# Graph and expert layers on one core: the tokens' way into the expert queues, and the experts' first layer

## The reference

```
msgs = layernorm(x)[src] * edge_weight[:, None]
x = x + segment_sum(msgs, dst) @ gnn_W.T + gnn_b
xf = layernorm(x)
probs = softmax(xf @ gate_w + gate_b)          # 8 experts
cw = the two largest of probs, else 0
for e in range(8):
    h = gelu(xf @ W1[e] + b1[e])               # 256 -> 512
    acc += cw[:, e] * (h @ W2[e] + b2[e])      # 512 -> 256
x = x + acc
```

## Time and profile before

| | us |
|---|---|
| median of 3 runs | 2954.43 (2953.14 to 2955.53) |
| profiled execution | 2958.51 |
| its span, first to last instruction | 2956.7 |
| PE busy | 2196.5 |
| POOL busy | 2013.2 |
| DVE busy | 1409.3 |
| ACT busy | 740.5 |

### The profile page before, as it was taken

How to read it: one execution, slowest core, us unless ns; L and a number is a source line. 1 busy time by engine, 2 the same in 40 slices (tenths; PEclk the granted TensorE clock), 3 DMA queues, 4 the chain that set the end, 5 groups by cost and what they waited for, 6 DMA issues and landing times.

```text
span 2956.7 us, 40846 instructions
## 1 busy us (share of the span) xinstructions
PE 2196.5 (74%) x9206; PEld 1482.4 (50%) x9207; DVE 1409.3 (48%) x5982; ACT 740.5 (25%) x1985; POOL 2013.2 (68%) x2107
## 2 busy tenths in 40 slices
PE   3656755984876977966966877978877887776695
PEld 2433533653654655644644654655555555544463
DVE  8855434453453443453454453443555555454422
ACT  3410200330221332321321221322322222222242
POOL 6657777777777777777777777777777777751121
PEclk8777977897988988988988987989998899887798
DMA  9663433443444443445555444434455564542423
GB/s 337 225 237 115 127 116 115 136 126 121 129 139 123 133 126 122 139 147 163 173 165 163 145 131 132 132 118 125 138 168 161 161 194 148 158 131 85 151 86 109
DMA packets 231445, 432.24 MB, mean 146 GB/s; under 512 B 47020, under 2 KB 158542, under 8 KB 228006
## 3 DMA queue, kind: packets, MB, share of 16 engines
q0 software_dynamic: 100368, 275.72, 31.3%
q1 hardware_dynamic: 128246, 144.38, 15.4%
q10 hardware_dynamic: 2592, 9.45, 0.8%
HBM read 326.80 MB, written 102.56 MB: 145 GB/s over the span
## 4 chain that ended last, share of the span: by engine, by line
POOL 50%; issue 20%; PE 15%; DVE 11%; DMA 3%; ACT 1%; ACTq 1%; DVEq 0%; SPq 0%; POOLq 0%
POOL rows L363 40%; POOL slots L391 5%; PE bank L599 5%; POOL results L396 5%; PE bank L685 4%; PE bank L667 3%; DVE spread L976 1%; DMA results<-y_sb,result_i 1%; PE bank L676 1%; DMA got<-results 1%; DVE y_sb L1154 1%; DVE item_t L1124 1%; DVE square_n L1023 1%; DVE pre_bn L932 1%; DVE bn L955 0%
## 5 line engine op out<-in xcount | busy, mean ns | idle before, releaser
L363 POOL DMA_INDIRECT rows<-xhat,src_t x1536 | 1470.0, 957 | 476.4 <-issue 464.4
L599 PE MATMUL bank<-rows,spread 128*80 128x256 f32 x3328 | 910.2, 435 | 324.8 <-issue 160.1
L599 PEld LDWEIGHTS bank<-rows,spread 128*80 128x80 f32 x3328 | 564.1, 175 | 607.6 <-issue 320.4
L685 PE MATMUL bank<-w,hT 128*128 x1848 | 489.1, 411 | 115.3 <-ACT hT L822 66.9
L685 PEld LDWEIGHTS bank<-w,hT 128*128 128x128 f32 x1848 | 366.2, 205 | 229.1 <-issue 180.9
L667 PE MATMUL bank<-w,xiT 128*128 x924 | 452.0, 612 | 11.6 <-ACT xiT L805 2.2
L989 DVE TENSOR_TENSOR acc<-acc,bank 128x160 f32 x208 | 67.0, 322 | 755.4 <-PE bank L589 730.3
L396 POOL DMA_INDIRECT results<-y_sb,result_i x231 | 226.8, 982 | 237.4 <-DVE y_sb L1157 181.3
L976 DVE TENSOR_SCALAR spread<-iota_w,dst_rel,wgt 128x80 f32<-128x80 f32 x1536 | 378.5, 340 | 0.2
L1153 DVE CAST result_i<-xi 128x1 int32 x231 | 35.1, 152 | 620.6 <-PE bank L685 339.1
L822 ACT ACTIVATE hT<-bank,b1T 128x128 f32<-128x128 f32 x924 | 263.4, 367 | 217.8 <-PE bank L676 212.2
(11 more groups left out here) (159 smaller groups left out, 1755.3 us busy)
## 6 DMA issues: line engine op xcount, KB each, us to landing
xi<-slots SPq DMA_DIRECT2D x231, 136.0 KB, 2.7
got<-results SPq DMA_DIRECT2D x97, 256.0 KB
rows<-xhat,src_t POOLq DMA_INDIRECT x1536
x_t<-in_x SPq DMA_DIRECT2D x97, 128.0 KB
x_d<-x_t SPq DMA_DIRECT2D x97, 128.0 KB, 2.3
res<-x_d SPq DMA_DIRECT2D x97, 128.0 KB
out_nodes<-res SPq DMA_DIRECT2D x97, 128.0 KB
w<-in_x SPq DMA_DIRECT2D x12, 1024.0 KB, 12.7
```

The source lines that it names most:

```text
L363: pool.indirect_dma_start(rows[q][:, c, :], None, x if g < RAW else xhat, bass.IndirectOffsetOnAxis(ap=src_t[:, g * CG + c:g * CG + c + 1] ...
L599: done = nc.tensor.matmul(B_SUM[0:W, 0:D], spread[g % 2][:, c, :], rows[q][:, c, :], start=c == 0, stop=c == CG - 1)
L685: done = nc.tensor.matmul(B_Y[:, 0:D], hT[i % 2][:, j, :], w2[:, bass.ds(e, 1), j, :].rearrange("p o f -> p (o f)"), start=j == 0, stop=j ...
```

## The change

Two things change together.

**Sort instead of scatter.** The two indirect sends per tile go. `place` additionally works out, for each tile, where each expert's run begins within the tile's 256 choices sorted by expert, and where it goes in the queues (`run_ends`). `mask_choices` (DVE) makes a 128 x 256 one-hot matrix from a tile's two places per node; `sort` (PE) multiplies it by the tile's rows in two halves, in the bank of `linear`; ACT copies each half; SP stores the 256 sorted rows in one of three staging areas in DRAM and, a turn later, copies 8 runs of 128 rows each (whatever their true length; later rows are overwritten) from DRAM to DRAM, after the previous tile's runs have landed. Mask, sort, stage and runs of a tile stand in four successive turns, one tile per turn.

**First weights per item, as the stationary side.** The first weights of an item's expert are loaded by SP with the item into one of 4 buffers, instead of all 8 experts' once. `up` makes 8 matmuls with a 128 x 128 block of weights as the stationary side and the turned item as the moving side (128 columns), which gives the output already turned, in one of two banks; `copy_h` and `turn_h` go, and `gelu` moves from item a to item b of a step, one step earlier.

To make room, the ring of node columns is 8 tiles instead of 16 and the normalisation has 6 buffers instead of 8.

```diff
-RING = 16
+RING = 8
...
+STAGE = 3 * P
+STAGES = 3
 XI = 6
 XB = 3
+W1B = 4
...
-LBUF = 8
+LBUF = 6
...
-        for _ in range(2 if busy else 4):
-            if send_next < NT and place_at.get(PART_OF[send_next], tau) < tau:
-                t.sends.append(send_next)
-                if send_next == PARTS[PART_OF[send_next]][1] - 1:
-                    sent_at[PART_OF[send_next]] = tau
-                send_next += 1
+        if turns:
+            t.sort, t.stage, t.runs = turns[-1].mask, turns[-1].sort, turns[-1].stage
+        if send_next < NT and place_at.get(PART_OF[send_next], tau + 1) <= tau:
+            t.mask = send_next
+            send_next += 1
+        if t.runs >= 0 and t.runs == PARTS[PART_OF[t.runs]][1] - 1:
+            sent_at[PART_OF[t.runs]] = tau
         open_to = max([sure_items(k) for k in sent_at if sent_at[k] < tau], default=0)
         waiting = open_to - item_next
-        n_steps = (1 + (waiting > 6 and tau % 2 == 0)) if busy else 1 if send_next < NT else 3
+        n_steps = (1 + (waiting > 6 and tau % 2 == 0)) if busy else 1 if NK - 1 not in sent_at else 3
...
-        w1, w2 = sb("w1", [P, NX, KD, H]), sb("w2", [P, NX, KH, D])
+        w1, w2 = sb("w1", [P, W1B, KD, H]), sb("w2", [P, NX, KH, D])
...
-            def send(t):
-                k, n = PART_OF[t], valid_rows(t)
-                pool.wait_ge(routed, k + 1)
-                for c in range(2):
-                    pool.indirect_dma_start(slots, bass.IndirectOffsetOnAxis(ap=slot_i[0:n, t, c:c + 1], axis=0),
-                                            xs[0:n, t % XR, :], None).then_inc(sent[k], 16)
...
+            def store_sorted(t):
+                if t >= STAGES:
+                    sp.wait_ge(runs_in, 16 * NX * (t - STAGES + 1))
+                sp.wait_ge(sorted_ready, 2 * t + 2)
+                sp.dma_start(stages[t % STAGES][0:2 * P].rearrange("(h p) f -> p h f", p=P), sorted_x[t % 2][:]).then_inc(staged[t % STAGES], 16)
+
+            def copy_runs(t):
+
+                k = PART_OF[t]
+                j = t - PARTS[k][0]
+                sp.wait_ge(routed, k + 1)
+                at = loaded_row(sp, run_ends[k % 2][:, j].rearrange("p c e -> p (c e)"))
+                sp.wait_ge(staged[t % STAGES], 16 * (t // STAGES + 1))
+                if t:
+                    sp.wait_ge(runs_in, 16 * NX * t)
+                if t in EPOCH_TILES[1:]:
+                    sp.wait_ge(tails_in, 16 * NX * EPOCH_OF[k])
+                for e in range(NX):
+                    a = nc.s_assert_within(at[e], 0, 2 * P, skip_runtime_bounds_check_because="a sum of a tile's counts")
+                    b = nc.s_assert_within(at[NX + e], 0, NX * S - 2 * P, skip_runtime_bounds_check_because="S holds every token")
+                    sp.dma_start(slots[bass.ds(b, P), :], stages[t % STAGES][bass.ds(a, P), :]).then_inc(runs_in, 16)
...
-                sp.wait_ge(routed, k + 1)
+                sp.wait_ge(runs_in, 16 * NX * PARTS[k][1])
...
-                    wait_sent(sp, k)
+                    sp.wait_ge(runs_in, 16 * NX * PARTS[k][1])
                     if ends_epoch(k):
                         sp.wait_ge(tails_in, 16 * NX * (EPOCH_OF[k] + 1))
...
+                b, e = loaded_row(sp, item_be[:, i])
+                b = nc.s_assert_within(b, 0, NX * BLOCKS - 1, skip_runtime_bounds_check_because="a block of the queues")
+                e = nc.s_assert_within(e, 0, NX - 1, skip_runtime_bounds_check_because="the block's expert")
                 if i >= XI:
                     sp.wait_ge(y_ready, i - XI + 1)
-                at = sp.value_load(item_b[:, i:i + 1], min_val=0, max_val=NX * BLOCKS - 1)
-                sp.dma_start(xi[i % XI][:], blocks[bass.ds(at, 1)].rearrange("o p f -> p (o f)")).then_inc(xi_in[i % XI], 16)
+                sp.dma_start(xi[i % XI][:], blocks[bass.ds(b, 1)].rearrange("o p f -> p (o f)")).then_inc(xi_in[i % XI], 16)
+                if i >= W1B:
...
                 else:
                     pe.wait_ge(x1_ready, t)
+                if n_sorted[0]:
...
+            def sort(t, h):
+                if h == 0:
+                    pe.wait_ge(mask_set, t + 1)
+                pe.wait_ge(x1_ready, n_linear[0])
+                if t or h:
+                    pe.wait_ge(sorted_ready, 2 * t + h)
+                nc.tensor.matmul(B_NODE[:, 0:XW], sort_mask[t % 2][:, h * P:(h + 1) * P], xs[:, t % XR, :],
+                                 start=True, stop=True).then_inc(sort_done, 1)
...
             def up(i):
+                pe.wait_ge(w1_in_sem[i % W1B], 16 * (i // W1B + 1))
+                pe.wait_ge(xiT_ready, i + 1)
+                if i >= 2:
+                    pe.wait_ge(hT_ready, i - 1)
+                for j in range(KH):
+                    for b in range(KD):
+                        done = nc.tensor.matmul(B_H[i % 2][:, j * P:(j + 1) * P], w1[:, i % W1B, b, j * P:(j + 1) * P], xiT[i % 2][:, b, :],
+                                                start=b == 0, stop=b == KD - 1)
+                done.then_inc(h_summed, 1)
...
+                    pe.wait_ge(w_in, 16 * NX)
                 pe.wait_ge(listed, part_of_item(i) + 1)
-                e = pe.value_load(item_e[:, i:i + 1], min_val=0, max_val=NX - 1)
-                pe.wait_ge(xiT_ready, i + 1)
-                if i:
-                    pe.wait_ge(h_ready, i)
-                for b in range(KD):
-                    done = nc.tensor.matmul(B_H[:], xiT[i % 2][:, b, :], w1[:, bass.ds(e, 1), b, :].rearrange("p o h -> p (o h)"),
-                                            start=b == 0, stop=b == KD - 1)
-                done.then_inc(h_summed, 1)
-
-            def turn_h(i):
-                pe.wait_ge(h_ready, i + 1)
-                if i:
-                    pe.wait_ge(hT_ready, i)
-                for j in range(KH):
-                    done = nc.tensor.transpose(B_HT[:, j * P:(j + 1) * P], h_sb[i % 2][:, j * P:(j + 1) * P], ident[:])
-                done.then_inc(h_turned, 1)
-
...
 
             def turns(plan, fast):
+                n_linear[0] = n_sorted[0] = 0
                 for t in plan:
-                    for a, b, _, _ in t.steps[:1]:
-                        step_up(a, b)
+                    for _, b, _, _ in t.steps[:1]:
+                        if b >= 0:
+                            up(b)
                     if t.add >= 0:
                         turn_sums(t.add)
+                    if t.sort >= 0:
+                        sort(t.sort, 0)
                     if t.gate >= 0:
                         turn_node(t.gate)
+                    for a, _, c, _ in t.steps[:1]:
+                        step_down(a, c)
+                    if t.sort >= 0:
+                        sort(t.sort, 1)
+                        n_sorted[0] = t.sort + 1
                     if t.linear >= 0:
                         linear(t.linear, fast)
-                    for a, _, c, _ in t.steps[:1]:
-                        step_down(a, c)
...
-                    act.dma_start(w1[:, e], w1_in[:, e]).then_inc(w_in, 16)
...
-                    wait_sent(act, PART_OF[t - XR])
+                    act.wait_ge(sort_done, 2 * (t - XR) + 2)
                 act.wait_ge(coef_ready, t + 1)
                 nc.scalar.activation(xs[:, t % XR, 0:D], x_t[t % XB][:], ACT.Identity,
                                      bias=shift[t % XB][:], scale=rstd[t % XB][:]).then_inc(xn_ready, 1)
+
+            def copy_sorted(t, h):
+                act.wait_ge(sort_done, 2 * t + h + 1)
+                if t >= 2 and h == 0:
+                    act.wait_ge(staged[(t - 2) % STAGES], 16 * ((t - 2) // STAGES + 1))
+                nc.scalar.activation(sorted_x[t % 2][:, h, :], B_NODE[:, 0:XW], ACT.Copy).then_inc(sorted_ready, 1)
...
-            def copy_h(i):
-                act.wait_ge(h_summed, i + 1)
-                if i >= 2:
-                    act.wait_ge(h_turned, i - 1)
-                nc.scalar.activation(h_sb[i % 2][:], B_H[:], ACT.Copy).then_inc(h_ready, 1)
...
-                act.wait_ge(h_turned, i + 1)
+                act.wait_ge(h_summed, i + 1)
                 if i >= 2:
                     act.wait_ge(y_summed, i - 1)
                 for j in range(KH):
-                    done = nc.scalar.activation(hT[i % 2][:, j, :], B_HT[:, j * P:(j + 1) * P], ACT.Gelu,
+                    done = nc.scalar.activation(hT[i % 2][:, j, :], B_H[i % 2][:, j * P:(j + 1) * P], ACT.Gelu,
                                                 bias=b1T[:, bass.ds(e * KH + j, 1)])
...
-                    for a, b, _, _ in t.steps[:1]:
-                        step_up(a, b)
+                    for _, b, _, _ in t.steps[:1]:
+                        if b >= 0:
+                            gelu(b)
+                    if t.sort >= 0:
+                        copy_sorted(t.sort, 0)
...
+                    if t.sort >= 0:
+                        copy_sorted(t.sort, 1)
...
+                offs = sort_off[:, 0:n * NX]
+                if k >= 2:
```

(57 more changed lines are left out.)

72 lines of the change are left out of this document (42 added, 30 removed).

## The result

The changed kernel takes 2975.15 us (median; 2972.63 to 2982.55, 4 runs) beside 2954.81 us (2953.14 to 2955.53) for the kernel before on the same chip: ratio 1.0069, interval 1.0055 to 1.0082. It is 0.7% slower. Forecast were 2829 us, within 2745 to 3110: the time lies inside the range, but the kernel became slower where it was forecast to become faster. Its profiled span is 2970.9 us, before 2956.7.

What follows compares the result with a forecast made beforehand. POOL (GpSimd) was taken as full until the last gather, PE next. Span: 2956.7 - 152 (last gather earlier) + 9 (turns behind) + 17 (closing steps) + 2 (start) = 2833, so 2829 us measured; range 2745 to 3110.

Steps and rivals of the forecast that it cites:

- What bounds before: Until the last gather at 2643 us POOL is full, at 1.25 us per transfer; PE is the next bound.
- Sends off POOL, -235 us: Gather stretch: removing 184 indirect sends frees 235.5 us of POOL; alone, the last gather would end at 2408 us.
- So the last gather ends at 2421 + 40 + 30 = 2491 us: End of gathers: PE's floor 2421, 40 for two equally full engines, 30 for transfers; 152 us earlier than before.
- VectorE, "nothing on the path, 22 us at most": Masks cost 75 us of a half-idle engine; only 17 placement turns add, at most 22 us, counted within the 40.
- Transfers, +30 us: Gather turns with a tile need 11.6 us of all transfer engines, not surely hidden: +30 us, ends 0 and +120.
- rival 2: Transfers become the bound, run bytes costing twice a load's: 3117 us or more; signs: long run waits, share above 0.85. Chance 0.24.
- Rival 1: POOL's floor is reached, PE's issue waits being POOL's doing and transfers costing nothing: 2750 us. Chance 0.18.
- SP, "it lies under those waits": SP's added issues, 6 us per tile's runs, 720 us in all, hide under its 1094 + 567 us waiting for VectorE.
- Behind the gathers, 165 us: After the last gather: 15 routing turns of 11 us instead of 12 of 13, +9 us (ends -20, +40).
- Weight loads: Up layer on PE: 16 load and matmul pairs at 0.11 us each, -0.4 us per item, -73 us over 182 items.
- Rival 3: Weight loads aren't hidden at 128 columns, 0.213 us a pair: PE's floor 2722, about 3120 us in all. Chance 0.07.
- Rival 4: The gain is eaten by SP's row loads near their upper end or the sort's waits: 2930 to 2970 us. Chance 0.09.

Runs made afterwards that it cites:

- e_w1_only: The kernel before, its indirect sends kept, with only the new up layer (first weights per item as stationary side): 2941.88 us.
- e_late_mask: The changed kernel with results scattered a turn later, four result buffers, and the first tile's mask ahead of the item list in placement turns: 2924.69 us.
- e_runs_bytes: The changed kernel with each run cut to the rows its expert can have on these inputs, 400 per tile instead of 1024: 2960.94 us.
- e_runs_16: The changed kernel with each run sent as two transfers of 64 rows, same bytes, 16 issues per tile instead of 8: 3474.35 us.
- e_fetch_act: The changed kernel with the combine's loads (x1 rows and result pairs) issued by ScalarE's queue at the end of its turn: 2962.55 us.
- e_mask_first: The changed kernel with the first tile's mask made before the item list, not behind it, in placement turns: 2961.71 us.
- e_late_mask_fetch: e_late_mask with the combine's loads also issued by ScalarE's queue: 2915.65 us, ratio 0.9867 to the kernel before.

## Why the prediction was wrong

- *What bounds before* stands: e_w1_only, with a shorter up layer, leaves the last gather where it was.
- *Sends off POOL, -235 us*: removed as said. TensorE's busy time stands too: 1853 us against 1874 - 73 + 82 = 1883 by my terms. Its waits don't: the floor of 2221 us leaves 2221 - 1883 = 338 us for them, and it was idle 532 of the 2385 us.
- **The failed step is "So the last gather ends at 2421 + 40 + 30 = 2491 us".** It came at 2584, 93 us late. I laid two engines' floors side by side and took 40 us for interplay, because before POOL hardly waited for anybody. But POOL scatters results between gathers in one order. With the sends it was nearly always later than VectorE's results (6 us of waits); without them it catches up with them and stalls (166 us), and with only three row buffers it stalls again when a turn is late (60 us). By the trace POOL's floor held as long as tiles were being sorted: in the bursts it is full. The time was lost in the turns between them, where 216 of the 227 us of waits lie and where VectorE's placements and the sums behind them come late. Moving the scatters and the mask brought back 41 of the 93 us (e_late_mask), in which POOL still waits 179 us for the sums. How the other 52 us divide among TensorE's waits for items, choices and results, no run separates.
- *VectorE, "nothing on the path, 22 us at most"*: the wait for masks is 124.7 us, since the first mask of a part stands behind placement and item list (up to 13.5 us), not beside six small operations. By the ratios the removal of most of it was worth 0.43% (13 us) alone and 0.58% (17 us) with late scatters; the wait itself overstated it.
- *Transfers, +30 us*: waits for items and weights are 109 us in the stretch, but by e_runs_bytes 61% of the runs' bytes were worth 0.42%, 12 us. The bytes were right (659 MB moved, 658 forecast). Of the two signs that I set for rival 2 one came, a share above 0.85 in turns with tiles (0.87), and one didn't: SP's waits for runs are 26 us, not hundreds. By its price, 314 us and more, rival 2 falls with e_runs_bytes, but a high share is no proof of a bound, nor is 0.87 free of charge. Rival 1 falls with POOL's waits.
- *SP, "it lies under those waits"*: this failed in its reason. The 6 us per tile that I took for issues and register row together are 6.0 for the issues alone; with the row (0.97 to 2.54 us, 1.52 in the median) and what surrounds it a tile takes 8.2 us in the stretch shown. And waits of 1094 + 567 us over the run said nothing of the tile turns, where SP waits 80 of 966 us. What spared the gathers, by the trace, is that POOL is full in the same turns. e_runs_16 shows the queue on the path for 0.82 of what is added; what it costs as it stands isn't shown, beyond that e_fetch_act moved no gather.
- *Behind the gathers, 165 us*: to the first closing step it took 213 us (2585 to 2798). The 15 turns were right, the 11 us were not: the kernel with the new weights alone has 138.0 / 12 = 11.5 us a turn up to the last tail, as I took it, and the sort makes 207.5 / 15 = 13.8 of it. 48 us over the forecast; with the 93 us above, this is the whole miss (2971 of span where 2833 were forecast). From 2585 to 2798 us TensorE waits in the changed kernel:

```profile
PE bank L718 <- DMA xi<-slots: 43.9, 5, 19.0
...
PE bank L680 <- DVE sort_mask L1190: 30.4, 5, 14.1
```

  Items wait for runs, tails (8 us) and landings on SP's queue, masks for the list. In this stretch there are no gathers to cover such waits. That the 48 us are these waits is read from the trace; of the single edits e_mask_first took 9 us from this stretch and e_fetch_act 5, and no run took most of it.
- *Closing steps, +17 us*: from the last tail on it is +16.2, of which three more steps at 4.49 us (forecast 4.6) are 13.5.
- *Weight loads*: 16 pairs in 1.85 us, 0.116 us a pair against 0.11 forecast. Rival 3 is dead: by the Trainium skill (TensorE: Matmul & The Clock Gate, "What overlaps and what doesn't") loads into the same row groups would not overlap the matmul; the trace disagrees at 128 columns as well, where the stream alone would be 0.107 us by the 0.427 for 512 columns. Rival 4 (2930 to 2970) came nearest, at 0.09: the sort's waits are among the causes, SP's row loads are not shown to be, and its price was still too low.

That the time lies inside the range is no merit of the working: the range was drawn up to 3110 for rivals 2 and 3, and neither of them came.

What stays open is the turns between the bursts. What holds the tile turns is POOL itself, in e_late_mask_fetch too: there only 22 of its 187 us of waits lie in the 13 bursts. Between them TensorE, VectorE's placements and the row buffers hold one another up, and the edits tried here moved the last gather by 41 us at most.

## What to carry to other kernels

Taking 235 us from a full engine buys no more than the chain behind it lets through, and an engine that works in one fixed order (gathers and scatters in turn) becomes a waiter as soon as it is the faster one: ask what it will wait for, and give that step a turn of distance and buffers together with the change. Ask it turn by turn: here the engine stayed full in the bursts of tiles and waited in the turns between them. Count a queue's issues in the same way, in the turns where they fall and with their register loads, not against its idle time over the run. A wait's size is not its worth: the 94 us of mask waits that went bought nothing in the gather stretch by themselves, and some 11 us of it once the scatters came late (2554.8 to 2543.5 us).

## What the runs showed of the hardware

- A transfer from DRAM to DRAM with two register addresses takes SP 0.775 us to issue (0.52 and its register work), eight 6.0 us, whether it carries 128 rows or 64 (changed kernel, e_runs_16); a plain load or store mostly 0.35 to 0.5 us. A load of sixteen registers takes 0.97 to 2.54 us, 1.52 in the median of 98 (line 348).
- Matmuls of 128 columns with a new 128 x 128 weight load each follow each other at 0.116 us at full clock (16 in 1.85 us), about the pitch of the transposes before (0.11 us).
- A busy share of the transfer engines of 0.87 over 13 bursts (0.70 in the mean of the stretch) is not yet a bound: with 61% less of the runs' bytes it was 0.76, the bursts were 4% shorter (966 to 929 us), and the kernel 0.4% faster.
